# Block-sparse attention stage: turned rows, q/k and v projections of the next batch moved to other groups

## The reference

```python
qkv = x @ w_qkv.T + b_qkv
q, k, v = jnp.split(qkv, 3, axis=-1)          # 16 heads of 16 columns
scores = jnp.einsum('bhqd,bhkd->bhqk', q * scale, k) + mask
attn = jax.nn.softmax(scores, axis=-1)
out = jnp.einsum('bhqk,bhkd->bhqd', attn, v)
return out.transpose(0, 2, 1, 3).reshape(B, L, D) @ w_out.T + b_out
```

## Time and profile before

| | us |
|---|---|
| median of 3 runs | 3202.59 |
| lowest and highest | 3199.77, 3204.59 |
| profiled execution | 3199.84 |
| its span, first to last instruction | 3198.0 |
| mean granted TensorE clock | 0.977 |

### The profile page before, as it was taken

One profiled execution on the slowest core, in us unless ns is written; L12 is line 12 of the kernel. 1 busy time (PEld: TensorE's weight loads), 2 busy tenths in 40 slices (PEclk: granted clock), 3 DMA queues, 4 the chain that ended last, 5 costly groups with the idle time before them and its releaser, 6 DMA issues. The chain is left out here.

```text
span 3198.0 us, 46175 instructions
## 1 busy us (share of the span) xinstructions
PE 3010.2 (94%) x14220; PEld 1742.7 (54%) x14220; DVE 2333.1 (73%) x4167; ACT 1702.7 (53%) x3501; POOL 1705.9 (53%) x1106
## 2 busy tenths in 40 slices
PE   6999999999999988899998799999999999999997
PEld 3354545454545444455554466666666666666665
DVE  8999999999999988577775455566655555565553
ACT  4767686858686753344444244444444444444442
POOL 2766666666666655233332555555555555565552
PEclk8999999999999999899999799999999999999999
DMA  4767676766667575211100000000001200000000
GB/s 141 260 210 262 214 249 217 244 221 246 231 231 249 204 235 200 89 40 39 39 21 27 20 16 5 20 20 20 20 20 40 73 14 21 25 26 26 26 13 20
DMA packets 131300, 343.37 MB, mean 107 GB/s; under 512 B 14898, under 2 KB 57990, under 8 KB 131222
## 3 DMA queue, kind: packets, MB, share of 16 engines
q1 hardware_dynamic: 128918, 334.02, 30.7%
q10 hardware_dynamic: 2304, 8.39, 0.7%
HBM read 320.87 MB, written 21.50 MB: 107 GB/s over the span
## 5 line engine op out<-in xcount | busy, mean ns | idle before, releaser
L559 POOL TENSOR_TENSOR hb<-bcB,du 128x1024 f32<-128x1024 f32 x256 | 602.5, 2354 | 390.1 <-DVE hb L699 351.0
L688 DVE TENSOR_TENSOR_SCAN ps_dA<-ps_dA,hb 128x1024 f32<-128x1024 f32 x256 | 585.7, 2288 | 44.8 <-ACT ps_dA L914 44.8
L1226 PE MATMUL ps_y<-hb,ident 128*128 128x512 f32 x1024 | 489.2, 607 | 29.9 <-DVE hb L699 29.8
L2323 POOL TENSOR_TENSOR c_pr<-c_pr,c_inv 128x512 f32<-128x512 f32 (+1 forms) x256 | 237.3, 935 | 322.7 <-DVE c_inv L2440 322.7
L914 ACT ACTIVATE ps_dA<-delta,a_neg 128x511 f32<-128x511 f32 x512 | 330.1, 676 | 1.1
L1226 PEld LDWEIGHTS ps_y<-hb,ident 128*128 128x128 f32 x1024 | 190.5, 193 | 252.9 <-issue 189.0
L699 DVE TENSOR_TENSOR hb<-ps_dA,bcC 128x1024 f32<-128x1024 f32 x256 | 311.9, 1218 | 5.9
L2576 ACT ACTIVATE c_pr<-c_ps_s,c_negmax 128x256 f32<-128x256 f32 (+1 forms) x512 | 224.0, 452 | 149.4 <-DVE c_negmax L2433 125.2
L1750 ACT ACTIVATE b_pt<-b_ps_t 128x512 f32<-128x512 f32 x320 | 174.1, 595 | 205.8 <-PE b_ps_t L1870 204.9
L2300 POOL TENSOR_TENSOR c_q_cos<-c_q_cos,c_q_sin 128x1024 f32<-128x1024 f32 x64 | 151.0, 2360 | 248.5 <-DVE c_q_sin L2410 246.7
L2433 DVE CUSTOM_DVE_ANT_0 c_ps_s<-c_ps_s,c_mask 128x256 f32<-128x256 f32 (+1 forms) x512 | 188.6, 418 | 122.3 <-issue 122.3
(11 more groups left out here) (304 smaller groups left out, 5921.9 us busy)
## 6 DMA issues: line engine op xcount, KB each, us to landing
bcB<-bc_scratch SPq DMA_DIRECT2D x256, 512.0 KB, 4.5
bcC<-bc_scratch SPq DMA_DIRECT2D x256, 512.0 KB, 4.6
c_x<-stream_scratch SPq DMA_DIRECT2D x16, 512.0 KB, 4.9
c_xr<-stream_scratch SPq DMA_DIRECT2D x16, 512.0 KB, 3.7
rows<-in_x_dram SPq DMA_DIRECT2D x8, 512.0 KB, 5.5
sum<-in_x_dram SPq DMA_DIRECT2D x8, 512.0 KB, 7.5
x_scratch<-sum SPq DMA_DIRECT2D x8, 512.0 KB, 7.0
b_xb<-x_scratch SPq DMA_DIRECT2D x8, 512.0 KB, 4.6
```

Source lines behind the costliest of these rows:

```text
L559: pool.tensor_tensor(hb[:, s % RING, :, :], bcB[:, s % ROWS, :, :], bc(du[:, c % 2, :].unsqueeze(1), [P, NG, T]), ALU.mult)\
L688: dve.tensor_tensor_scan(flat(h_all), flat(h_all), flat(tile), 0.0, ALU.mult, ALU.add)\
L1226: last = pe.matmul(ps_y[:, :], W["ident"][:, :], hb[:, r % RING, i, :], start=False, stop=(g == GROUPS - 1 and i == NG - 1))
L2323: pool.tensor_tensor(rows, rows, bc(inv[:, u, :].unsqueeze(2), [P, 2, w]), ALU.mult)\
```

## The change

In pass m=0 the four transposes of the next batch's rows go to groups 0 (one), 1 (two) and 2 (one); q of half 0 is projected in group 3, k in group 5. In pass m=1, q of half 1 is projected in group 1 and k in group 3. The v projection is made of two halves, in groups 4 and 5 of pass m=1. VectorE takes v after the maximum of its group 5 instead of group 4, and computes the statistics of the batch after the next after that of group 6 instead of group 5. ScalarE's copies follow the ring.

```diff
+        def turned_at(m, k):
+            return () if m or k > 2 else ((0,), (1, 2), (3,))[k]
+        def projected_at(m, k):
+            return (0,) if k == (1 if m else 3) else (1,) if k == (3 if m else 5) else ()
...
-                    if more and m == 0 and k in (3, 4):
-                        uses += [("x", 2 * (k - 3)), ("x", 2 * (k - 3) + 1)]
-                    if more and k == 5:
-                        uses += [("qk", m, 0), ("qk", m, 1)]
+                    if more:
+                        uses += [("x", h) for h in turned_at(m, k)] + [("qk", m, keys) for keys in projected_at(m, k)]
...
-                    if more and k == 4:
-                        take_v(n)
                     if k == 7:
                         divide(b, 0)
-                    if more2 and k == 5:
+                    if more and k == 5:
+                        take_v(n)
+                    if more2 and k == 6:
                         statistics(n + 1)
...
-                        if more and m == 0 and k in (3, 4):
-                            for h in (2 * (k - 3), 2 * (k - 3) + 1):
+                        if more:
+                            for h in turned_at(m, k):
                                 take_x(b + 1, h, b, uses["x", h])
-                        if more and k == 5:
-                            for keys in range(2):
+                            for keys in projected_at(m, k):
                                 take_qk(b + 1, m, keys, b, uses["qk", m, keys])
...
-            def project_v(n):
-                for t in range(TT):
+            def project_v(n, ts):
+                for t in ts:
...
-                last.then_inc(v_proj.s, 1)
+                if ts[-1] == TT - 1:
+                    last.then_inc(v_proj.s, 1)
...
-                    if more and k in (3, 4):
-                        for h in (2 * (k - 3), 2 * (k - 3) + 1):
+                    if more:
+                        for h in turned_at(0, k):
                             turn_x(n, h, b, uses["x", h])
-                    if more and k == 5:
-                        for keys in range(2):
+                        for keys in projected_at(0, k):
                             project_qk(n, 0, keys, b, uses["qk", 0, keys], uses["x", 3])
...
                     if more and k == 4:
                         pe.wait_ge(max_ready.s, max_ready.at(n, 6))
-                        project_v(n)
+                        project_v(n, (0, 1))
                     if more and k == 5:
-                        for keys in range(2):
+                        project_v(n, (2, 3))
+                    if more:
+                        for keys in projected_at(1, k):
                             project_qk(n, 1, keys, b, uses["qk", 1, keys], uses["x", 3])
```

## The result

| | before | after |
|---|---|---|
| median of 20 runs | 3203.51 us | 3211.16 us |
| lowest and highest | 3199.71, 3209.74 | 3205.00, 3212.58 |
| ratio | | 1.0022, 95% interval 1.0015 to 1.0029 |
| profiled execution, span | 3199.84, 3198.0 | 3211.58, 3209.8 |

The forecast was +1.7 us with a range of 3198 to 3211.5. The median of after lies inside that range, at its upper end, 7.65 us over before. By the forecast's own bounds (slower over 3209.0) this is "slower", to which it had given 0.17, though barely: the interval of the ratio reaches from 0.15% to 0.29%.

The account below looks back on a forecast made before the run. TensorE's own order, plus short waits for ScalarE's ring and one for VectorE, bound the stage. Steady batch 0.0 + 1.24 - 0.82 = +0.42; 6 x 0.42 - 0.82 = +1.7 us, forecast 3204.3 us, range 3198 to 3211.5.

Parts of the forecast that it names:

- (a): Pass m=1 up to slot 6: q/k projections and v halves between slots remove two ring stalls, 1.58 us saved.
- (b): Slot 6 of pass m=1: TensorE waits for the later v copy, 1.56 us newly idle; with (a), 0.0.
- (c): Before slot 8: statistics behind maximum 8 make maximum 9 late, +1.24 us on TensorE, in six batches.
- (d): Pass m=0, slots 1 to 6: earlier row transposes and separated q and k projections, -0.82 us a batch.
- The rule weighed: VectorE's norm: lockout with a GpSimd instruction could cost some 0.5 us more per batch, +3 in all.
- The clock: Slower rival: TensorE's two waits per batch lower its clock, 1.5 us lost a batch, +10.7 us, 3213.3; chance 0.03.
- the forecast's main case: Whole kernel: +1.7 us, 3204.3 us, with the clock staying at 1.00; chance 0.76.
- the first slow rival: Pass m=0 gives nothing back, so a batch costs 1.24 us more: +7.4 us, 3210.0; chance 0.13.
- The statistics weren't hidden: Faster rival, before slot 8: VectorE's statistics are hidden, maximum 9 isn't late, -5.7 us, 3196.9; chance 0.05.
- the copy only: Faster rival, slot 6: the v copy is hidden as well as the statistics, 3185.9 us; chance 0.03.
- a dearer release after a long wait: At three places per batch: a release costing more than 0.13 us after a long wait would break the sum.

Follow-up runs that it names:

- run 3: Kernel before with only the statistics moved, behind maximum 8 instead of maximum 7: period 57.50 us (+1.19), median 3205.23 us, ratio 1.0011.
- run 5: Changed kernel with the statistics back behind maximum 7 and the v copy: period 56.31 to 56.39 us, median 3198.69 us, ratio 0.9996.
- run 1: Kernel before with only the m=0 part of the change (row transposes, q and k of half 0): period 55.80 us, median 3195.99 us, ratio 0.9986.
- runs 7 and 8: Spare transposes added in the last batch's pass m=1, to the changed kernel (3200.94 us, ratio 0.9995) and to the kernel before (3194.48 us, ratio 0.9975).
- run 9: Changed kernel with v whole in group 4, copy and statistics as before, and m=1's q after slot 3, k after slot 5: 3191.35 us, ratio 0.9967.
- run 2: Kernel before with only q and k of half 1 moved to groups 1 and 3 of pass m=1: period 56.30 to 56.33 us, ratio 0.9993.
- run 4: Changed kernel with the v projection whole in group 4, its copy and the statistics where they were before: median 3195.59 us, ratio 0.9977.
- run 6: Kernel before with v in halves after slots 4 and 5, copy behind maximum 7, q/k pair still behind the second half: 3202.41 us, ratio 0.9999.

## Why the prediction was right or wrong

**The range and the direction of the sum** held: more lost before slot 8 than m=0 gives back. But the size was off, +1.7 us forecast for the batches and 5.1 to 6.5 measured with the last batch's clock held. The median lies 0.34 us inside the range. The width of the range kept it there, not the sum, so the hit is partly luck. The range isn't the sum of its parts either: -3 to +7.5 and 2.4 of spread around 3202.59 make 3197.2 to 3212.5.

**(a) and (b), m=1 up to slot 6: forecast 0.0, measured +0.33** (1510.99 to 1527.58 is 16.59, against 16.26). The wait was priced well: from the start of the second v half to slot 6 it was 3.40, the sum had 1.825 + 1.56 = 3.39. The stalls of slots 1 to 4 went as said. The term that was mis-sized is the filler. I took half of a pair, 1.815 for a projection and 1.825 for half of v. Standing alone they take 1.92 (1512.07 to 1513.99) and 1.93 (1521.17 to 1523.10). Two alone are 3.84 where the pair was 3.63, so each block costs about 0.2 beyond its matmuls, and the sum had charged half of that to a half. Three such blocks stand before slot 6, 0.1 over their term each: 0.3. Why a block costs this, no run shows.

**(c), the statistics: forecast +1.24, measured +1.19** (slot 6 to slot 8: 1527.58 to 1532.98 is 5.40, against 4.21), and +1.19 again alone in run 3. This step was right in place and size. In the ladder it is +0.97, as run 5 has a small wait of its own at slot 8. The wait itself was forecast at about 1.6 and is 1.30, since the 0.4 named for before is about 0.14 (swap 1529.39 + 1.13, slot 8 at 1530.66).

**(d), m=0: forecast -0.82, measured -0.47** (1540.23 to 1554.02 is 13.79, against 14.26; 1540.23 is the weigh step at 1539.23 plus 1.00), and -0.51 alone in run 1. The wait for norm was as said (0.19 idle, 0.26 forecast from TensorE's readiness). The rest is again the single blocks: two projections at 1.91, and two transposes at 0.37 instead of 0.30. That row, 1543.73 to 1544.10, had been in the forecast; I took it for a start after a wait, but row 3's transposes, with no wait before them, take the same 0.37.

Together 0.33 + 1.19 - 0.47 = +1.05 per batch instead of +0.42; the period says +1.04. Put into the forecast's own sum, the measured terms give 6 x 1.05 + 0.33 - 0.47 = +6.2 us instead of +1.7, near the 6.5 of runs 7 and 8.

**The rule weighed** added nothing to the sum: norm still takes 1.75 us, one of its four instructions still up to 0.79, and TensorE's wait for it was no longer than the rows said. The Trainium skill (SBUF — State Buffer, Who interferes with whom) has the loser blocked for the other's whole instruction; the estimate from it, up to 0.5 us more, didn't come true in this trace.

**The clock.** The rival stood in the wrong place. The two waits of 1.4 and 1.3 us in the steady batches left the granted clock at 1.00, as the forecast's main case had it:

```profile
1505.25:1562.60 57.35, 53.94 (x456) 29.78 (x452) 43.24 (x53) 26.76 (x50) 18.87 (x19) 1.00 0.12 37
```

The early fall came in the last batch, in untouched code, and cost the profiled execution 5.67 us plus much of the 2.0 behind it. The chance of that was missing from the rivals: the earlier trace rows covered a steady batch, and I didn't read the last one, where the profile before shows the 0.69 and the 5.79 us output projection. Spare work in the idle places held the clock at 1.00 there. With that the trace agrees with the Trainium skill (TensorE: Matmul & The Clock Gate, What's actually happening), by which activity releases the throttle. The early fall isn't this change's alone: in the profiled executions the tail was 32.66 in the kernel before and in runs 1, 3 and 9, 35.89 and 35.90 in runs 2 and 4, 37.54 in run 6, 38.33 in the changed kernel and 41.37 in run 5, all with the same code in the last batch. How often it falls early, and whether this change makes that likelier, stays open. Of the 7.65 us between the medians, 6.5 are seen with the last batch's clock held, and so about 1 is left for it, which is less than these medians resolve.

**Rivals.** The m=0 pass did give something back, so the first slow rival was wrong, although its total (3210.0) is close to the result. It got there with another mechanism. The forecast had named a period of 57.5 as that rival's sign, and 57.35 came; the period alone would have misled, and only run 1 tells the two apart. The statistics weren't hidden (run 3), and the copy only where the pair was left behind it (run 6). What I named as able to break the sum, a dearer release after a long wait, costs nothing extra here, since the stretch up to slot 6 is as long as its terms. But slot 6 behind the wait takes 1.32 (1527.58 to 1528.90) instead of 1.09, and that is hidden under the wait before slot 8.

## What to carry to other kernels

Before an instruction block is moved away from a place, ask whose cover it was: the pair of projections filled TensorE's ring and hid two VectorE blocks, and only the first was visible as a stall. A filler cut into pieces fills more gaps but costs more in all (here about 0.2 us for one piece more, 3.84 against 3.63), so cut it only into as many pieces as there are stalls that are clearly longer. Look at distances between starts too: a loss can be missing from the list of waits, as slot 6's in run 2. And for a difference of 0.2%, compare intervals of the program (here, output projection to output projection) and look at the granted clock of the stage's last, thin part, before a median is believed.

## What the runs showed of the hardware

The TensorE clock can fall at different points of the same code: the last batch's tail took from 32.66 us (kernel before) to 41.37 (run 5). And one and the same kernel spends different times at the lower clock: run 1's eleven executions spread over 13 us (3192.6 to 3205.9), in clusters that go with the mean clock (0.978, 0.976, 0.972 to 0.973). Matmuls whose results nobody reads removed the early fall: 54 transposes in the waits of one batch brought the kernel before down by 9 us against its median beside it (3203.44 to 3194.48), more than the 4 us that I expected, probably because the median execution of before has a lower mean clock (0.974) than the profiled one (0.977). A lone q or k projection (four matmuls of 512 columns in the trace) takes 1.92 us between two slots, and 1.815 in a pair.
